# Second attention: probabilities turned by VectorE in 32x32 blocks and moved by DMA, instead of transposed by TensorE

## The reference

```
x = x + cross_attention_0(layernorm(x), ctx)        # 16 heads of 8
x = x + ffn_0(layernorm(x))                         # 8 experts, the best 2 of each token
x = x + cross_attention_1(layernorm(x), ctx)        # 16 heads of 64, low-rank additions
x = x + ffn_1(layernorm(x))                         # 16 experts, each takes its best 32 tokens per sequence pair
```

```
q_in = x @ Wq + lora_q;  k_in = org @ Wk + lora_k;  v_in = org @ Wv + lora_v
out  = attention(q_in, k_in, v_in) + attention(q_in, ipa @ Wk_ipa, ipa @ Wv_ipa)
return out @ Wo + bo + lora_o
```

## Time and profile before

| | |
|---|---|
| Median of three runs | 516.61 us |
| Profiled execution: span from first to last instruction | 513.1 us |
| around the span | about 3.5 us (516.61 less 513.1) |
| TensorE busy | 487.3 us, 95% |
| VectorE, ScalarE, GpSimd busy | 354.2, 288.2, 234.4 us |
| Second attention, from the first score of batch 0 to the end of round 16 | 135.16 to 392.83 us |
| Granted TensorE clock, mean | 0.989 |

### The profile page before, as it was taken

One profiled execution on the slowest core, in us unless ns is written; L12 is line 12 of the kernel. 1 busy time (PEld: TensorE's weight loads), 2 busy tenths in 40 slices (PEclk: granted clock), 3 DMA queues, 4 the chain that ended last, 5 costly groups with the idle time before them and its releaser, 6 DMA issues.

```text
span 513.1 us, 13570 instructions
## 1 busy us (share of the span) xinstructions
PE 487.3 (95%) x5109; PEld 378.7 (74%) x5113; DVE 354.2 (69%) x1000; ACT 288.2 (56%) x984; POOL 234.4 (46%) x331
## 2 busy tenths in 40 slices
PE   4799999998999999999999999899999999999996
PEld 3466766656668778887787777788757897799995
DVE  5888989766786678566786665757866588535553
ACT  3366566463586776666867657665664444413332
POOL 4845545035365544575444755324231980090440
PEclk9699999999999999999999999999999999999999
DMA  8900000000001100111000000022202100000001
GB/s 229 234 3 4 3 3 3 3 1 8 4 1 32 34 20 16 34 33 34 3 2 2 4 3 3 1 66 64 64 0 71 56 0 1 1 22 24 1 2 42
DMA packets 21872, 14.48 MB, mean 28 GB/s; under 512 B 5928, under 2 KB 21136, under 8 KB 21808
## 3 DMA queue, kind: packets, MB, share of 16 engines
q1 hardware_dynamic: 20704, 13.31, 9.6%
q10 hardware_dynamic: 1104, 0.30, 0.3%
HBM read 12.30 MB, written 1.05 MB: 26 GB/s over the span
## 4 chain that ended last, share of the span: by engine, by line
PE 79%; DVE 12%; ACT 3%; issue 2%; DMA 1%; POOL 1%; ACTq 0%; DVEq 0%; POOLq 0%
PE bank L1792 9%; PE bank L1721 6%; PE bank L1551 5%; PE bank L1558 5%; PE bank L1801 5%; PE bank L1538 5%; PE bank L1510 5%; PE bank L1374 5%; PE bank L1463 5%; PE bank L1521 4%; PE bank L1530 4%; PE bank L1808 3%; PE bank L1609 3%; PE bank L1359 3%; ACT work L1150 2%
## 5 line engine op out<-in xcount | busy, mean ns | idle before, releaser
L1150 ACT ACTIVATE work<-bank,negmax 128x124 f32<-128x124 f32 x256 | 90.0, 387 | 52.2 <-DVE ipa_s L775 52.0
L498 POOL TENSOR_TENSOR work<-work,rsum 128x496 f32<-128x496 f32 x64 | 64.1, 1012 | 120.2 <-DVE rsum L789 120.2
L533 POOL TENSOR_SCALAR work<-work,slot 128x128 f32<-128x128 f32 x64 | 49.7, 792 | 48.3 <-DVE slot L864 29.4
L1150 ACT ACTIVATION_READ_ACCUMULATOR work<-bank,negmax 128x1 f32 x256 | 58.9, 230 | 0.0
L1792 PE MATMUL bank<-work 128*128 128x256 f32 x224 | 53.4, 381 | 0.0
L1014 DVE SCALAR_TENSOR_TENSOR work<-work,bank 128x256 f32<-128x256 f32 x64 | 26.9, 421 | 33.0 <-ACT work L1302 32.8
L1302 ACT ACTIVATE work<-bank 128x256 f32<-128x256 f32 x64 | 24.5, 383 | 40.6 <-PE bank L1792 29.1
L481 POOL TENSOR_TENSOR work<-work 128x512 f32<-128x512 f32 (+2 forms) x48 | 39.2, 817 | 12.1 <-DVE work L745 9.6
L306 DVE TENSOR_TENSOR x_all<-bank,x_all 128x128 f32<-128x128 f32 x16 | 4.7, 292 | 57.4 <-PE bank L1721 55.4
L1792 PEld LDWEIGHTS bank<-work 128*128 128x128 f32 x224 | 40.3, 190 | 4.7 <-DVE work L1017 0.2
L773 DVE TENSOR_REDUCE negmax<-bank 128x4 f32<-128x496 f32 x64 | 42.5, 664 | 0.0
(11 more groups left out here) (197 smaller groups left out, 1101.1 us busy)
## 6 DMA issues: line engine op xcount, KB each, us to landing
work<-in_L_ffn_w_dram SPq DMA_DIRECT2D x42, 128.0 KB, 2.3
x_all<-in_x_dram SPq DMA_DIRECT2D x4, 256.0 KB, 5.8
out_dram<-x_all SPq DMA_DIRECT2D x4, 256.0 KB, 2.6
ctx_all<-in_ctx_dram SPq DMA_DIRECT2D x4, 192.0 KB, 6.0
ctx_all<-in_L_ffn_w_dram SPq DMA_DIRECT2D x6, 128.0 KB, 2.3
work<-in_L_xattn_Wq_dram SPq DMA_DIRECT2D x1, 512.0 KB, 6.5
work<-in_L_xattn_Wo_dram SPq DMA_DIRECT2D x1, 512.0 KB, 8.2
work<-in_L_ffn_We_dram SPq DMA_DIRECT2D x1, 512.0 KB, 5.7
```

What stands on the lines that cost most here:

```text
L498: pool.tensor_tensor(part, part, rsum1[:, b % 2, CH * n:CH * n + CH].unsqueeze(2).broadcast_to((128, CH, ORG)), ALU.mult).then_inc(Z.norm, 1)
L533: ins = pool.tensor_scalar(ohw_of(e)[:, k, :], count[:, :], slot[:, h, 0, k, e % E1:e % E1 + 1], slot[:, h, 1, k, e % E1:e % E1 + 1], ALU. ...
L1150: ins = act.activation(p1[:, b % 2, n, c, 0:ORG], blocks(bank[n])[:, c, 0:ORG], ACT.Exp, bias=negmax1[:, b % 2, h:h + 1], accum_out=sums1[ ...
```

## The change

For batches 0 to 13 TensorE no longer transposes the probabilities. VectorE turns each 128x128 head in 32x32 blocks (`turned_in_blocks`), four heads per instruction, from `p1` buffer 0 into what was `p1` buffer 1, arranged by column block. A block then lies on the wrong partitions: block (row q, column k) sits in partitions of q and belongs in those of k. Sixteen DMAs per batch, 32 partitions by 2 KB each, carry them there (`p1T`, now arranged as the earlier trace rows). The DMAs are issued by SP once all four turns of a batch are done; `outputs` waits until all sixteen have landed (`Z.moved`, 16 per DMA). Probabilities therefore have one buffer until batch 14: `powers` waits for the turn of the same four heads of the batch before, the first turn of a batch for the moves of the batch before. Batches 14 and 15 are transposed by TensorE as before, in functions of their own (`last1`).

The orders are rewritten. TensorE's round: first scores, first queries, second scores, projection of batch `b - 2` (a round later than before), second queries, first FFN product, both keys, second FFN product, both outputs, first values, input, second values. The second keys go to bank 5 rather than 6, outputs of batches 0 to 13 to banks 4 and 6, the two values exchange banks.

```diff
-        p1T = work.take([128, H, S])
+        p1T = work.take([128, 4, H, 32])
+        turned_blocks = p1[:, 1, :, :, :].rearrange("p n c s -> p (n c s)").rearrange("p (k h j) -> p k h j", k=4, h=H)
...
+        MOVES = 16 * 16
+        def p_of(b):
+            return p1[:, 1 if b == B - 1 else 0, :, :, :]
+        def head_T(h):
+            return p1T[:, :, h, :]
...
@@ SP, loop over f
                 sp.dma_start(v1[ORG:S, f % 2, :], ipa_v[IPA * f:IPA * f + IPA, :]).then_inc((Z.vi0, Z.vi1)[f % 2], 16)
+                if 1 <= f <= LAST_TURNS:
+                    sp.wait_ge(Z.blocks, CH * f)
+                    for k in range(4):
+                        for q in range(4):
+                            sp.dma_start(p1T[tile_rows(k), q, :, :], turned_blocks[tile_rows(q), k, :, :]).then_inc(Z.moved, 16)
...
@@ VectorE
+            def turned_in_blocks(b, n):
+                dve.wait_ge(Z.norm, CH * b + n + 1)
+                dve.wait_ge(Z.ipa_p, b + 1)
+                after(dve, Z.moved, MOVES * b)
+                dve.transpose(turned_blocks[:, :, CH * n:CH * n + CH, :].rearrange("p k h j -> p h k j"),
+                              p_of(b)[:, n, :, :].rearrange("p h (k j) -> p h k j", k=4)).then_inc(Z.blocks, 1)
...
             def round1(b):
+                f, y, g = b + 1, b - 2, b + 4
+                if there(b):
+                    for n in range(CH):
+                        shifted(b, n)
                     summed(b, 0)
...
+                if there(y):
+                    residual1(y)
...
                 if there(g):
                     weighted(g, bank[7])
                 if there(b):
+                    for n in range(CH - 1):
+                        turned_in_blocks(b, n)
                     summed(b, 3)
...
                 if there(b + 3):
                     xn1_of(b + 3)
+                if there(b):
+                    turned_in_blocks(b, CH - 1)
...
@@ ScalarE
             def powers(b, n):
                 act.wait_ge(Z.maxed, CH * b + n + 1)
+                if b < B - 1:
+                    after(act, Z.blocks, CH * (b - 1) + n + 1)
+                else:
+                    act.wait_ge(Z.moved, MOVES * LAST_TURNS)
...
             def round1(b):
+                queries(f, 0)
+                if there(b):
+                    powers(b, 1)
+                    powers(b, 2)
+                    ipa_powers(b)
...
+                queries(f, 1)
                 if there(g):
                     weighted(g, bank[7])
                 if there(b):
+                    powers(b, 3)
...
@@ TensorE
             def outputs(t, n, freed, count):
-                for k in (2 * n, 2 * n + 1):
-                    pe.wait_ge(*p_copied(t, k))
+                if t < LAST_TURNS:
+                    pe.wait_ge(Z.moved, MOVES * (t + 1))
+                else:
+                    for k in (2 * n, 2 * n + 1):
+                        pe.wait_ge(*p_copied(t, k))
...
+            def project(t):
+                pe.wait_ge(Z.o_sb, 2 * t + 2)
+                for c in range(8):
+                    mm = pe.matmul(bank[7][:, 0:D], o1T[:, c, :], wo1[:, c, :], start=(c == 0), stop=(c == 7))
+                mm.then_inc(Z.proj, 1)
...
             def round1(b):
                 if there(b):
                     scores(b, 0)
...
+                queries(f, 0, Z.v_sb, 2 * f - 1)
+                if there(b):
+                    scores(b, 1)
...
+                if there(y) and not j:
+                    project(y)
+                queries(f, 1, Z.v_sb, 2 * f)
...
+                after(pe, Z.x_new, y + 1)
...
                 if there(g):
                     ffn(g, 0, bank[7])
+                keys(f, 0, Z.o_sb, 2 * t)
...
+                keys(f, 1, Z.q_sb, 2 * f + 1)
...
                 if there(g):
                     pe.wait_ge(F.ys0, g + 1)
                     ffn(g, 1, bank[7])
                 if there(t):
+                    outputs(t, 0, Z.q_sb, 2 * f + 2)
+                    outputs(t, 1, Z.k0_sb, f + 1)
...
+                values(f, 0, Z.k1_sb, f + 1)
...
                     inputs(b + 2)
+                values(f, 1, *((Z.o_sb, 2 * t + 1) if there(t) else (Z.q_sb, 2 * f + 2)))
```

More of the change, by code:

```diff
@@ L981, in round1, with round1_14, last1 @@
                     added(10, 1)
+            def round1_14():
+                for n in range(CH):
+                    shifted(LAST_TURNS, n)
+                summed(LAST_TURNS, 0)
+                residual1(LAST_TURNS - 2)
+                eight(0, 1)
+                summed(LAST_TURNS, 1)
+                dve.wait_ge(Z.k0, B)
+                dve.tensor_copy(k1T[:, (B - 1) % 2, 0:4, 0:ORG], bank[6][:, 0:4 * ORG].rearrange("p (c n) -> p c n", c=4))\
+                    .then_inc(Z.k0_sb, 1)
+                summed(LAST_TURNS, 2)
+                eight(0, 2)
+                ipa_norm(LAST_TURNS)
+                summed(LAST_TURNS, 3)
+                eight(0, 3)
+                places(0)
+                slot_weights(0)
+            def last1(b):
+                t = b - 1
+                if there(b):
+                    shifted(b, 0)
+                turned(t, 0)
+                if b == B:
+                    onehot(5)
+                if there(b):
+                    residual1(t - 1)
+                    shifted(b, 1)
+                    onehot(0)
+                    summed(b, 0)
+                    shifted(b, 2)
+                turned(t, 2)
+                onehot(1 if there(b) else 6)
+                if there(b):
+                    shifted(b, 3)
+                onehot(2 if there(b) else 7)
+                if there(b):
+                    summed(b, 1)
+                    onehot(3)
+                    summed(b, 2)
+                    summed(b, 3)
+                    ipa_norm(b)
+                    onehot(4)
+                else:
+                    normalize(xn_half[1], HB, 12, rstd_at["half", 1], R.xn)
+                    normalize(xn_half[1], 12, B - 1, rstd_at["half", 2], R.xn)
+                residual1(t)
+                if there(b):
+                    rstd_at["half", 2] = variances(Z.stats, B - 1, 12, B - 1)
             for b in range(-4, B + 2):
@@ L1294, in _ @@
                     inputs(0)
-            for b in range(-1, B + 1):
+            for b in range(-1, B - 1):
                 round1(b)
+            last1(B - 1)
+            last1(B)
             def tanh(e, c):
@@ L1665, in round1 @@
                     fold(6)
-                if there(t):
-                    turn(t, 3, *((Z.q_sb, 2 * f + 2) if there(f) else p_copied(t, 0)))
+                if b == 12:
+                    route_hidden(0, bank[7])
+                keys(f, 1, Z.q_sb, 2 * f + 1)
+                if b == -1:
+                    fold(7)
+                    fold(8)
                 if b == 13:
                     route_logits(0, bank[7])
-                if b == 15:
-                    gather(1)
-                    tell(2, G.xg, 1)
                 if there(g):
```

328 lines of the change are left out of this document (132 added, 196 removed).

## The result

The changed kernel takes 547.08 us (median of 4 runs, 543.95 to 548.53), the kernel before 515.88 beside it (4 runs, 514.41 to 516.74). The ratio is 1.0593, 95% interval 1.0557 to 1.0629: slower by 31 us. The prediction was 496.8, its range 488 to 513; rival C (527) had the sign and the place, and too little. The profiled execution took 547.65 us, its span is 545.8, 32.7 longer than before.

What follows compares the result with a forecast made beforehand. TensorE bounds the kernel before; afterwards the transfers set the round at 13.65 us, by a hair over TensorE's 13.38. From 516.6, changes of -1.2, -12.9, -7.6 and +1.9 (together -19.8) give 496.8 us; range 488 to 513, likeliest 491 to 503.

Steps and rivals of the forecast that it cites:

- rival C: At SP: moves issued at the SBUF-to-SBUF row's pitch of 0.64 make rounds of 16.2, 527 us; chance 0.14.
- The gain: TensorE, batches 0 to 13: without transposes it loses 26.0 us, a round of TensorE alone becomes 13.38 us.
- The turn: VectorE: a four-head block turn costs 0.60 us like the PSUM copy, one pass; upper bound 1.20.
- The issue: SP: moves issued every 0.47 us, as loads over 32 rows, the last 7.05 us behind the first.
- Landing: DMAs: the last move of a batch lands in 2.05 us, the middle of 1.8 and 2.3.
- The loop: VectorE and DMAs: moves landed to next first turn, taken as 0.7 us shorter than the loop through the outputs.
- The loop through the outputs: TensorE's outputs wait for the moves: blocks there at 23.29 us, outputs 9.64 into a round, so a round of 13.65.
- The value rows: SP: the next batch's value rows and weight loads stand behind the moves and cost nothing.
- T's loop: Follow-up theory, not the prediction's: the one buffer of turned blocks closes the loop that sets the round, 16.6 us.
- The start: Ahead of batch 0: first scores stay at 135.16 us; the sum counts changes only from there.
- B: DMAs: landing under load makes the loop about 1 us longer, P = 14.65, 507 us; chance 0.18.
- A: TensorE is the bound everywhere, the chain 0.3 us better, all 26 us come out, 490 us; chance 0.12.

Runs made afterwards that it cites:

- experiment 4: Changed kernel with 8 transfers per batch in place of 16, the other half of the outputs' input a constant: 499.87 us, 0.9697 of the kernel before.
- the table's last column: Stretch times of the last follow-up: changed kernel with 12 transfers, four GpSimd copies, reordered VectorE work, early second FFN product, one block buffer: 497.91 us.
- experiment 1: Changed kernel with the same 16 transfers reading a weight matrix in device memory: 516.04 us, 0.9993 of the kernel before.
- 2: Changed kernel with half of the bytes in each of the 16 transfers (rows of 1 KB): 542.9 us, 1.0513 of the kernel before.
- Experiment 3: Changed kernel with a second buffer of turned blocks: 538.06 us, 1.0384 of the kernel before.
- 5: Changed kernel with VectorE reordered: fourth group's reciprocal before the third turn, other work between third and fourth turns after the fourth: 531.83 us, 1.0281 of the kernel before.
- 9: Changed kernel with 16 transfers reading device memory, a second buffer of turned blocks and VectorE's work reordered: 501.63 us, 0.9715 of the kernel before.
- experiment 10: Changed kernel with all 16 transfers, two buffers of turned blocks, VectorE's work reordered and the early second FFN product: 520.98 us, 1.0081 of the kernel before.
- experiment 6: Changed kernel with the second FFN product ahead of the second keys again in the round before batch 0: 544.22 us, 1.0526 of the kernel before.
- 11: Changed kernel with 12 transfers, four GpSimd copies, VectorE's work reordered, early second FFN product, one buffer of turned blocks: 497.91 us, 0.9649 of the kernel before.

## Why the prediction was wrong

**The gain was right.** TensorE alone needs 13.58 us a round (experiment 4), 13.38 was predicted. With the transfers out of the way the stretches come out as predicted, within 1.4 us each (the table's last column, where the transfers are shortened). Whether each small term kept in the sum was right is not shown.

**The turn was right.** "I take the copy's 0.60": a mean of 0.689, three in 1.90 us, so one pass and not two. The sentence of the Trainium skill that the prediction cites there ("Vector Engine (DVE) Microarchitecture Reference", "The reshape front-end and per-opcode configuration", one element per cycle per lane) agrees with it.

**The issue: failed.** "I take 0.47, since that row has the shape of the moves ... and the other only the kind of memory." Of the two things that told the rows apart it was the kind that mattered: the same shape costs 0.421 from device memory and 0.591 from SBUF (experiment 1), and half of the bytes leave it at 0.591 (2). The nearest row was the earlier trace rows, though its 4 partitions looked unlike; it gave 0.64, measured is 0.63. On top comes one long issue in most batches (1.42 us in the one shown), which no term held. Of the 3.1 us that the way is longer there, 15 x 0.16 = 2.4 are the price and about 0.8 the long issue. Landing was right: 2.04 for 2.05. Taking the price away by the source brings 547.1 to 516.0.

**The loop: failed.** "The other loop (moves landed, next first turn) is 0.7 shorter, because no weighting is in it." It starts at the landing and holds three turns, a reciprocal, a normalisation and the fourth turn, 3.96 us (3.70 by the prediction's own terms), none of it beside the transfers: round = way + 3.96. The loop through the outputs, which the prediction took for the longest, has two rounds in it, because a late output also shifts the scores behind it: half of (14.04 + way + 3.74), the last term the outputs' 1.90 and the values' 1.84. The first grows with the whole way and the second with half, so the order depends on the way: at 9.25 they give 13.2 and 13.5, at 12.34 they give 16.3 and 15.1. Bounding the way from both sides and then working with one loop alone is what hid this. Experiment 3 shows it with 9 us. Experiments 5 and 9 cut more than this loop, and their 15 and 14.4 us hold for the loops together.

**The value rows: failed.** The prediction saw them stand behind the moves, where "they cost nothing". Ahead of the next moves they are a third loop: SP's copy waits for the outputs of the batch before, and those for their transfers. The way of 12.34, the outputs, 0.63 for the copy and 0.17 of handovers make 15.1 us with outputs of 1.97, and 16.6 with outputs of 3.46. In the changed kernel it holds the moves of batches 1, 7 and 12 by 0.3 to 0.6 us, on top of T's loop; where T's loop is cut, it comes out (3 and 10).

**The start: failed.** The sum begins at the first score. But in the round ahead of it the second FFN product was moved behind the second keys and the foldings, too, and batch 0's scores wait for VectorE's sums behind it (L790, which end at 140.28):

```profile
131.44 1.13 PE L1521 MATMUL bank<-work 128*128 128x512 f32 x2
...
134.48 2.05 PE L1542 MATMUL bank<-work 32*128 32x128 f32 x16
140.38 1.87 PE L1568 MATMUL bank<-work 64*128 64x128 f32 x14 [3.85 <-issue]
...
139.00 1.28 DVE L790 TENSOR_TENSOR work<-bank,work 128x512 f32<-128x512 f32 x2
```

"No work is added to TensorE" is true, but the order changed. 5.2 us in the trace; experiment 6 got about 3 of them back.

**The rest.** 547.08 less 31.04 (experiment 1), 14.41 (9) and the 3.72 between experiments 9 and 11 is 497.91; 1.1 above the forecast is left. (9 and 11 also differ in their transfers, so the 3.72 is not the start alone.)

**The rivals.** *C* was it: the right place (SP), the right row, and a point of decision (1.6 us more way) that was passed with 3.1. Its signs came, issues of 0.591 us and an idle of 2.63 us before outputs. Its 16.2 a round came from the loop through the outputs counted over one round, which gives 14.8 counted rightly; that it lay near the measured 16.6 is luck. Its 527 lacked the long issues, the start, and the work of batches 3, 4 and 9 to 11 ahead of their fourth turn (rounds of 17.5 to 18.8). The chance of 0.14 rested on weighing shape over kind. *B*'s limit by the data is not what binds: half of the bytes saved 0.2 us of landing and left every issue as it was. The rule of the Trainium skill on port halves that stood beside it ("SBUF — State Buffer", "Door 1: The DMA port swizzle") has no row here for or against it. *A* needs a way shorter than predicted, which with sixteen transfers only single batches of experiments 1 and 9 had (8.9 to 9.2 us).

## What to carry to other kernels

Price a DMA issue by the row that shares its two memories, and count issues on one queue like instructions on an engine: sixteen of them are 10 us. For each buffer that the change makes single, write the loop that starts at its release and ends at its next release; compare all loops at both ends of every unknown, since their order can change in between. Look also at what stands ahead of a transfer in its queue, and what that waits for. When a block exchange is made of transfers, look first for the blocks that need not travel. Whether a second engine's queue could have taken half of the issues was not tried.

## What the runs showed of the hardware

An issue of an SBUF-to-SBUF transfer held SP for 0.591 us with rows of 1 KB and of 2 KB over 32 partitions, and 0.60 for 4 partitions; from device memory 0.421 for the same shape. The Trainium skill ("DMA: Bandwidth & Descriptors", "Anatomy of one DMA — SWDGE (gpsimd) path") says of transfers issued by GpSimd that most of their fixed cost of about 2 us is completion and not set-up. The landing of 2.04 us here, of a transfer issued by SP, is as long; but the completion overlapped from one transfer to the next, and the issue was what added up.

In most batches one issue took longer, 1.42 us in the one shown and 1.78 at most, from device memory as well (maximum 1.89). The page lists a queue for instructions beside those for data:

```profile
q8 instruction: 40, 0.66, 0.5%
```

Its packets, 16 KB each, stand in the trace with their times. In the changed kernel 13 of the 224 issues took over 0.9 us (the others at most 0.82), and each of them starts 0.08 to 0.30 us after such a packet does. In the twelve kernels with moves there are 144 such issues, and none starts farther than 0.41 us from one. So the long issue goes together with a load of instructions; how that holds SP was not tried.

The clock: in the changed kernel the outputs took 3.28 to 3.68 us in 7 of 14 batches, each after a wait of 2.36 to 5.90, and 1.97 in the others, some after waits of 1.5 to 3.6. Two windows, one inside each kind of outputs:

```profile
270.87:272.50 1.63, 1.63 (x16) 1.63 (x18) 1.55 (x3) 0.00 (x0) 0.00 (x0) 0.50 0.78 228
...
287.51:289.40 1.89, 1.89 (x32) 1.73 (x32) 1.81 (x3) 0.60 (x1) 0.00 (x0) 1.00 0.00 0
```

0.50 is the lower level, 1.2 GHz, and 1.00 the upper; the idle time ahead was 2.63 and 1.50 us. With one buffer this cost little: the round with outputs of 3.46 took 16.58 and the one before it, with 1.97, took 16.39. TensorE is not in T's loop, and the slow outputs reach the next moves only through the value rows, 0.3 us late. Where T's loop is cut they cost more (experiment 10).
